# Self-attention on one NeuronCore: one exponential of two PSUM banks in place of two of one bank

## The chip, the cores and the metric

The kernel runs on 1 core of one Trainium2 chip. The metric is the device time of one execution in microseconds. Lower is better. Three runs of the kernel before gave 3151.02, 3143.84 and 3139.68 us, median 3143.84.

## What is computed

A decoder of two layers on x of 4 x 512 tokens x 512. Each layer is attention, cross-attention and feed-forward, each with a residual and a layer norm. The change is in the self-attention, which both layers have (`L0_attn`, `L1_attn`); it is one function, called twice:

```
x = _layernorm(x + _L0_attn_ref(x, ...))      # self-attention, layer 0
x = _layernorm(x + _L0_xattn_ref(x, ctx_512, ctx_512))
x = _layernorm(x + _L0_ffn_ref(x, ...))
x = _layernorm(x + _L1_attn_ref(x, ...))      # self-attention, layer 1
...
# self-attention, 16 heads of 32, B=4, S=512:
q, k, v = (split_heads(x @ W.T + b) for W, b in ((Wq, bq), (Wk, bk), (Wv, bv)))
scores = einsum('bhqd,bhkd->bhqk', q, k) * HEAD_DIM ** (-0.5)
scores = where(causal, scores, -inf)
out = einsum('bhqk,bhkd->bhqd', softmax(scores), v)
return out.reshape(B, S, HIDDEN) @ Wo.T + bo
```

## The kernel before, in words

`stage_self_attention` works in 16 groups n: batch element b = n // 4, and in it four heads, g = n % 4. One list, `plan` (lines 169 to 195), gives the order of all work, and each engine walks it and does its own part of each entry, in order. In the loop over groups, a group's entries are:

- `S n s`, s = 0 to 4: one **T unit**. TensorE writes scores, keys on the partitions, of the four heads into T, a PSUM tile of two banks of 512 columns (lines 487 to 500), and ScalarE takes them through the exponential to PT in SBUF (lines 298 to 307). `EXP_UNITS` (line 205) says which blocks of which head lie where; units 0 and 1 have two score matmuls, one a bank; the others have four, two a bank. Each score matmul (line 497) is followed by one that adds the causal mask (line 499).
- `M max (n+1, u)`, u = 0 to 5: a **maximum unit** of the next group. TensorE writes its scores, queries on the partitions, into one of two tiles M of two banks (lines 476 to 481), and VectorE reduces them to row maxima (line 375). These stand between the T units: two behind s=0, two behind s=1, one each behind s=2 and s=3.
- `M qk n+2`: the projections of the group after the next (line 422), taken from M by ScalarE (lines 291, 292) and VectorE (lines 364, 366) to HL, from which six DMAs of the SP queue and six of the POOL queue stack them to QKS (lines 221 to 223). `M mt n+1` transposes the maxima; a DMA of the ACT queue brings them to QKS (line 296).
- `P n 0..2`: the product of PT with V and with ones, into O and DEN (line 517). `Q`, `R`: VectorE's reciprocal of DEN and its multiplication (lines 393, 395), and the split of the result into two parts (lines 314, 399).
- in certain g, `xt` (transposed x), `v` (values) and `out` (output projection) units through M.

The last group, n=15, has no maximum units, so its five T units stand in a row. Groups 14 and 15 have no `qk` unit.

There is one tile T. Two semaphores pass it back and forth. TensorE, for each bank k of unit s:

```
t.wait_ge(t_free, 2 * (5 * n + s) + k + 1)
```

and it raises `t_full` behind the last matmul of each bank. ScalarE:

```
for k in range(2):
    bank = slice(BANK * k, BANK * (k + 1))
    act.wait_ge(t_full, 2 * (5 * n + s) + k + 1)
    ac.activation(PT[:, s, bank], T[:, bank], ACT.Exp, scale=SCALE).then_inc(t_free, 1)
```

Counts of `t_free` also release the PV products (line 509), and `t_full` the DMAs of HL (line 217). Both count two a unit.

Of the kernel before, what the change touches and what calls it, by code (L numbers as in the profile page):

```python
# [10 lines left out]
ACT = mybir.ActivationFunctionType  # L11
# [8 lines left out]
BANK = 512  # L20
# [90 lines left out]
def stage_self_attention(nc, tag, X, C, wts, bias_qk, bias_rows, x_src=None):  # L111
# [10 lines left out]
    SCALE = HD ** -0.5  # L122
    MOMENTS = NT + RSTD_STEPS
    pe, ve, ac, gp = nc.tensor, nc.vector, nc.scalar, nc.gpsimd
    ctx = ExitStack()
    with ctx:
# [12 lines left out]
        PT = sb("PT", [P, 5, 2 * BANK], F32)  # L139
# [12 lines left out]
        T = ps("T", [P, 2 * BANK])  # L152
# [8 lines left out]
        t_full, t_free = sem("t_full"), sem("t_free")  # L161
# [65 lines left out]
        @block.sync  # L227
        def _(sp):
            if x_src is not None:
                sp.dma_start(X[:, 0, :, :], x_src[:, 0, :, :]).then_inc(x_in, 16)  # L230
            sp.dma_start(WS[0], wts[0]).then_inc(w_in[0], 16)
            sp.dma_start(WS[1], wts[1]).then_inc(w_in[1], 16)
            sp.dma_start(BQK[:], bias_qk).then_inc(b_in, 16)
            sp.dma_start(BR[:], bias_rows).then_inc(b_in, 16)
            for w in range(2, 4):
                sp.wait_ge(w_lo, w - 1)
                sp.dma_start(WS[w % 2], wts[w]).then_inc(w_in[w % 2], 16)
            sp.wait_ge(ones_set, 2)
            for n in range(GROUPS):
                stack(sp, n, (0, 2))  # L240
                if x_src is not None and 1 <= n < NB:
                    sp.dma_start(X[:, n, :, :], x_src[:, n, :, :]).then_inc(x_in, 16)
# [25 lines left out]
        @block.scalar  # L268
        def _(act):
            act.sem_inc(t_free, 2)  # L270
            for x in plan:
                if x[0] == "W":
                    w = x[1]
                    act.wait_ge(w_in[w % 2], 16 * (w // 2 + 1))
                    ac.activation(WH[:, w], WS[w % 2], ACT.Copy).then_inc(w_hi, 1)
                elif x[0] == "M" and x[1] == "xt":
                    half = x[2][1]
                    act.wait_ge(m_full, at["xt", x[2]] + 1)
                    ac.activation(XTH[:, 2 * half:2 * half + 2, :].rearrange("p k s -> p (k s)"),
                                  M[at["xt", x[2]] % 2][:], ACT.Identity).then_inc(hi_done, 1)  # L280
                elif x[0] == "M" and x[1] == "qk":
                    n = x[2]
                    c = n % G
                    src = M[at["qk", n] % 2]
                    act.wait_ge(m_full, at["qk", n] + 1)
                    if n == 0:
                        act.wait_ge(b_in, 32)
                    else:
                        for arrived in stacked[(n - 1) % 2]:
                            act.wait_ge(arrived, 16 * 3 * ((n - 1) // 2 + 1))  # L290
                    ac.activation(HL[:, 1, :], src[:, 0:BANK], ACT.Identity, bias=BQK[:, 0, c:c + 1])
                    ac.activation(HL[:, 2, :], src[:, BANK:], ACT.Identity, bias=BQK[:, 1, c:c + 1]).then_inc(hi_done, 1)
                elif x[0] == "M" and x[1] == "mt":
                    n = x[2]
                    act.wait_ge(m_free, drained("mt", n))
                    act.dma_start(QKS[R:R + 1, n % 2, 0, :, :].bitcast(F32).rearrange("p h (i q) -> p (h i) q", i=NT),
                                  mT[:, :].bitcast(F32)).then_inc(shifted, 16)
                elif x[0] == "S":
                    n, s = x[1:]
                    if n == 0:  # L300
                        act.wait_ge(w_lo, 4)
                    else:
                        act.wait_ge(pv_part, 3 * (n - 1) + EXP_READER[s] + 1)
                    for k in range(2):
                        bank = slice(BANK * k, BANK * (k + 1))
                        act.wait_ge(t_full, 2 * (5 * n + s) + k + 1)
                        ac.activation(PT[:, s, bank], T[:, bank], ACT.Exp, scale=SCALE).then_inc(t_free, 1)  # L307
                elif x[0] == "Q":
                    n = x[1]
                    b, g = n // G, n % G  # L310
                    act.wait_ge(o_free, n + 1)
                    if b >= 1:
                        act.wait_ge(m_full, at["out", (b - 1, 1)] + 1)
                    ac.activation(ATH[:, g, :], AQ[:], ACT.Identity).then_inc(at_hi, 1)
# [1825 lines left out]
```

## Time and profile before

| | |
|---|---|
| median of 3 runs | 3143.84 us (3139.68 to 3151.02) |
| the profiled execution, its own time | 3156.45 us |
| its span, first to last instruction | 3154.7 us |
| mean granted clock of TensorE | 0.825 of full |
| busy: TensorE matmul / weight load | 2211.2 us / 1507.4 us |
| busy: VectorE / ScalarE / GpSimd | 1897.6 us / 1173.2 us / 527.9 us |
| the exponentials of self-attention | 320, 179.2 us busy, 596 ns each |
| TensorE waiting for them | 5.9 us, 16 times |

Times are from the start of the span. Engines are PE (TensorE matmul), PEld (its weight load), DVE (VectorE), ACT (ScalarE), POOL (GpSimd) and SP. A group of instructions is given with its line in the kernel, out<-in tiles, form, count, busy time and the mean of one, and then the engine's idle time before it with what ended it. In a timeline "x2" is two instructions that follow each other, shown as one with their common length; the matmuls' ends are modelled. The granted clock is 1.00 at full and 0.50 at half.

### The profile page before, as it was taken

To read this page: it belongs to the slowest core of one execution; us is meant where nothing else is said; L and a number is where in the kernel's file an instruction comes from. 1 tells how busy PE (TensorE), PEld (TensorE's weight loads), DVE (VectorE), ACT (ScalarE), POOL (GpSimd) and SP (SyncE) were. 2 spreads that over 40 slices of the span, in tenths; PEclk is the share of its full clock that TensorE was granted. 3 is DMA by queue.
4 is the path that set the end of the run, shared out by engine and by line. 5 is a ranking of instruction groups with operands and counts; after the bars stand their busy time and mean duration, and the time that the engine had idled before them with its cause. 6 is when DMAs were issued, how large, how long until landed. Compare 5 with 4: busy or idle time off the path is not lost. (4 is left out here: it accounts for less than half of the span.)

```text
span 3154.7 us, 35002 instructions
## 1 busy us (share of the span) xinstructions
PE 2211.2 (70%) x12378; PEld 1507.4 (48%) x12410; DVE 1897.6 (60%) x3060; ACT 1173.2 (37%) x2000; POOL 527.9 (17%) x498
## 2 busy tenths in 40 slices
PE   6999997578788328888848999995001638777770
PEld 5777775222222115555427777772001627655550
DVE  3355555578778556666653455554888343488876
ACT  2222221266666423333322222221785112255550
POOL 1112122101011000000001112211000040266654
PEclk7798998699999669999966889897555569999995
DMA  4222120521321210000012212210000200399875
GB/s 127 68 61 61 41 61 21 129 64 36 78 63 37 107 67 0 0 0 0 0 61 60 61 41 61 61 41 15 0 0 0 96 1 0 129 305 303 300 240 160
DMA packets 79911, 233.25 MB, mean 74 GB/s; under 512 B 16688, under 2 KB 17968, under 8 KB 70960
## 3 DMA queue, kind: packets, MB, share of 16 engines
q0 software_dynamic: 23552, 121.67, 12.9%
q1 hardware_dynamic: 55216, 109.70, 12.4%
q8 instruction: 78, 1.28, 0.2%
q10 hardware_dynamic: 1024, 0.26, 0.0%
q14 instruction: 41, 0.34, 0.0%
HBM read 149.23 MB, written 31.50 MB: 57 GB/s over the span
## 5 line engine op out<-in xcount | busy, mean ns | idle before, releaser
L773 DVE TENSOR_REDUCE x_negm<-x_M 128x2 f32<-128x1024 f32 x256 | 309.0, 1224 | 78.8 <-PE x_M L833 78.0
L307 ACT ACTIVATE L_attn_PT<-L_attn_T 128x512 f32<-128x512 f32 x320 | 179.2, 596 | 461.9 <-PE L_attn_T L499 461.8
L729 ACT ACTIVATE x_PT<-x_T 128x512 f32<-128x512 f32 x512 | 278.5, 598 | 185.2 <-PE x_T L853 179.9
L375 DVE TENSOR_REDUCE L_attn_negm<-L_attn_M 128x2 f32<-128x1024 f32 (+1 forms) x192 | 195.4, 1044 | 169.5 <-PE L_attn_M L480 169.0
L478 PE MATMUL L_attn_M<-L_attn_QKS 96*128 96x256 f32 (+3 forms) x512 | 195.5, 439 | 49.6 <-DMA L_attn_QKS<-L_attn_HL 27.4
L497 PE MATMUL L_attn_T<-L_attn_QKS 97*128 97x384 f32 (+3 forms) x512 | 193.2, 436 | 12.5 <-DMA L_attn_QKS<-L_attn_mT 10.5
L853 PE MATMUL x_T<-x_QS,x_KS 49*128 49x512 f32 x512 | 137.1, 532 | 46.7 <-ACT x_PT L729 41.6
L1310 PE MATMUL graph_P<-ident,graph_L 128*128 128x128 f32 x64 | 15.7, 427 | 214.0 <-DVE graph_L L1383 208.7
L221 POOL DMA_DIRECT2D L_attn_QKS<-L_attn_HL x64 | 34.8, 543 | 747.5 <-DVE L_attn_mT L379 669.0
L478 PEld LDWEIGHTS L_attn_M<-L_attn_QKS 96*128 96x128 f32 x512 | 123.4, 241 | 71.7 <-DVE L_attn_negm L375 15.1
L862 PE MATMUL x_O<-x_PT,x_V 128*32 128x512 f32 x1024 | 150.3, 662 | 8.3 <-issue 8.3
L1331 ACT ACTIVATE graph_seen_a<-graph_SIM,graph_mid 128x512 bf16<-128x512 f32 x200 | 141.4, 709 | 34.6 <-DVE graph_mid L1363 34.6
L833 PE MATMUL x_M<-x_KS,x_QS 48*128 48x512 f32 x512 | 114.8, 446 | 39.6 <-DVE x_negm L773 20.3
L853 PEld LDWEIGHTS x_T<-x_QS,x_KS 49*128 49x128 f32 x512 | 51.0, 196 | 189.5 <-ACT x_PT L729 136.0
L480 PE MATMUL L_attn_M<-mask_qk,identr 128*128 128x128 f32 x512 | 138.5, 276 | 0.0
L499 PE MATMUL L_attn_T<-mask_kq,identr 128*128 128x128 f32 x512 | 136.4, 274 | 0.0
L1366 DVE TENSOR_SCALAR_CACHE_REDUCE graph_seen_v<-graph_SIM,graph_mid 128x512 bf16<-128x512 f32 x200 | 135.3, 742 | 0.9
L1859 ACT ACTIVATE slots_WH<-slots_RAW 128x1024 fp32r<-128x1024 f32 x94 | 94.6, 1054 | 110.8 <-DMA slots_RAW<-in_experts,slots_PICK 110.8
L497 PEld LDWEIGHTS L_attn_T<-L_attn_QKS 97*128 97x128 f32 x512 | 123.7, 242 | 20.3 <-DMA L_attn_QKS<-L_attn_mT 12.1
L1920 DVE TENSOR_TENSOR slots_WL<-slots_RAW,slots_WH 128x1024 fp32r<-128x1024 f32 x48 | 128.7, 2681 | 0.2 <-ACT slots_WH L1871 0.2
L499 PEld LDWEIGHTS L_attn_T<-mask_kq,identr 128*128 128x128 f32 x512 | 125.0, 244 | 0.2
L480 PEld LDWEIGHTS L_attn_M<-mask_qk,identr 128*128 128x128 f32 x512 | 124.8, 244 | 0.3
(365 smaller groups left out, 5462.6 us busy)
## 6 DMA issues: line engine op xcount, KB each, us to landing
L_attn_QKS<-L_attn_HL SPq DMA_DIRECT2D x192, 128.0 KB, 4.8
L_attn_QKS<-L_attn_HL POOLq DMA_DIRECT2D x192, 128.0 KB, 3.7
moe_y_rows<-slots_YS SPq DMA_DIRECT2D x48, 256.0 KB
x_QS<-x_xh SPq DMA_DIRECT2D x128, 64.0 KB
X<-in_x SPq DMA_DIRECT2D x4, 1024.0 KB
x_xh<-x_XTH SPq DMA_DIRECT2D x4, 1024.0 KB, 3.9
x_xl<-x_XTL SPq DMA_DIRECT2D x4, 1024.0 KB, 5.1
x_KS<-x_ch SPq DMA_DIRECT2D x32, 128.0 KB, 4.5
```

The lines of the kernel that those rows point to most:

```text
L307: ac.activation(PT[:, s, bank], T[:, bank], ACT.Exp, scale=SCALE).then_inc(t_free, 1)
L375: last = ve.tensor_reduce(negm[:, g % 2, h0:h0 + nh, i], src, AX.X, ALU.max, negate=True)
L478: pe.matmul(m[:, c:c + w], QKS[0:R, r, 0, h, P * i:P * (i + 1)], QKS[0:R, r, 1, h, 0:w], start=True, stop=False)
L480: last = pe.matmul(m[:, c + P * i:c + w], C["identr"][:], C["mask_qk"][:], start=False, stop=True)
L497: pe.matmul(T[:, c:c + w], QKS[0:R + 1, r, 1, h, P * j:P * (j + 1)], QKS[0:R + 1, r, 0, h, P * j:S], start=True, stop=False)
L499: last = pe.matmul(T[:, c:c + P], C["identr"][:], C["mask_kq"][:], start=False, stop=True)
L729: ac.activation(PT[:, s // 4, head(s), :], T[(STEPS_S * g + s) % 3][:], ACT.Exp, scale=SCALE).then_inc(t_free, 1)
L773: ve.tensor_reduce(negm[:, g % 2, u // 4:4:2, u % 4], m[:].rearrange("p (r k) -> p r k", r=2), AX.X, ALU.max, negate=True).then_inc(m_free, 1)
L853: pe.matmul(T[(STEPS_S * g + s) % 3][:], KS[rows, g % KV, P * j:P * (j + 1)], QS[rows, g % 4, head(s) % 2, :], start=True, stop=True).then ...
L862: last = pe.matmul(O[VW * h:VW * (h + 1), :], V[:, (g // KV) % 2, j, g % KV, :], PT[:, j, h, :], start=(j == 0), stop=(j == NT - 1))
L1331: inst = ac.activation(seen_a[:, t - DVE_TILES, :], SIM[:, t, :], ACT.Sign, scale=-1.0, bias=mid[:, t:t + 1], accum_out=count[:, t:t + 1])
L1366: inst = ve.tensor_scalar(seen_v[:, t, :], SIM[:, t, :], mid[:, t:t + 1], 0.0, ALU.is_ge, ALU.add, accum_out=count[:, t:t + 1])
```

## The change

ScalarE waits until both banks of a T unit are full, takes both with one exponential of 1024 columns, and adds 2 to `t_free` when it ends. What is computed is the same. TensorE's code, with its waits for each bank, stays as it is; as both counts now come together, the wait for the second bank is met with the first. Nothing else is changed.

```
--- before
+++ after
@@ -301,10 +301,8 @@
                         act.wait_ge(w_lo, 4)
                     else:
                         act.wait_ge(pv_part, 3 * (n - 1) + EXP_READER[s] + 1)
-                    for k in range(2):
-                        bank = slice(BANK * k, BANK * (k + 1))
-                        act.wait_ge(t_full, 2 * (5 * n + s) + k + 1)
-                        ac.activation(PT[:, s, bank], T[:, bank], ACT.Exp, scale=SCALE).then_inc(t_free, 1)
+                    act.wait_ge(t_full, 2 * (5 * n + s) + 2)
+                    ac.activation(PT[:, s, :], T[:], ACT.Exp, scale=SCALE).then_inc(t_free, 2)
                 elif x[0] == "Q":
                     n = x[1]
                     b, g = n // G, n % G
```

## Rows read from the trace of the kernel before

**Rows 1.** The page, part 2: busy tenths of the matmul engine and its granted clock, in 40 slices.

```profile
PE   6999997578788328888848999995001638777770
...
PEclk7798998699999669999966889897555569999995
```

**Rows 2.** Groups of instructions, then one line's view: line 307, line 279.

```profile
L307 ACT ACTIVATE L_attn_PT<-L_attn_T 128x512 f32<-128x512 f32 x320 | 179.2, 596 | 461.9 <-PE L_attn_T L499 461.8
...
L279 ACT ACTIVATE L_attn_XTH<-L_attn_M x16: 1004/1025/1046, 15.9 to 1982.3; 128x1024 fp32r<-128x1024 f32 x16
```

**Rows 3.** Timeline, group n=3, full clock: start us, us, engine, line, instruction.

```profile
169.46 0.39 PE L497 MATMUL L_attn_T<-L_attn_QKS 97*128 97x384 f32 x1
...
169.86 0.28 PE L499 MATMUL L_attn_T<-mask_kq,identr 128*128 128x128 f32 x1
...
170.23 1.08 ACT L307 ACTIVATE L_attn_PT<-L_attn_T 128x512 f32<-128x512 f32 x2 [1.89 <-PE L_attn_T L499]
...
170.37 0.27 PE L499 MATMUL L_attn_T<-mask_kq,identr 128*128 128x128 f32 x1
...
171.42 0.39 PE L497 MATMUL L_attn_T<-L_attn_QKS 97*128 97x384 f32 x1
...
171.64 0.22 PE L499 MATMUL L_attn_T<-mask_kq,identr 128*128 128x128 f32 x1
...
172.33 0.27 PE L499 MATMUL L_attn_T<-mask_kq,identr 128*128 128x128 f32 x1
...
173.34 0.34 PE L497 MATMUL L_attn_T<-L_attn_QKS 97*128 97x256 f32 x1
```

**Rows 4.** Timeline, group n=7 at the low clock.

```profile
286.06 0.63 PE L497 MATMUL L_attn_T<-L_attn_QKS 97*128 97x384 f32 x1
...
287.77 0.41 PE L499 MATMUL L_attn_T<-mask_kq,identr 128*128 128x128 f32 x1
...
288.22 0.60 ACT L307 ACTIVATE L_attn_PT<-L_attn_T 128x512 f32<-128x512 f32 x1 [0.30 <-PE L_attn_T L499]
...
289.69 0.63 PE L497 MATMUL L_attn_T<-L_attn_QKS 97*128 97x384 f32 x1
```

**Rows 5.** Timeline, the last group of layer 0, n=15.

```profile
507.01 0.50 PE L497 MATMUL L_attn_T<-L_attn_QKS 97*128 97x512 f32 x1
...
507.70 0.23 PE L499 MATMUL L_attn_T<-mask_kq,identr 128*128 128x128 f32 x1
...
508.33 0.50 PE L497 MATMUL L_attn_T<-L_attn_QKS 97*128 97x512 f32 x1 [0.40 <-ACT L_attn_PT L307]
...
508.98 1.08 ACT L307 ACTIVATE L_attn_PT<-L_attn_T 128x512 f32<-128x512 f32 x2 [0.22 <-PE L_attn_T L499]
...
509.63 0.44 PE L497 MATMUL L_attn_T<-L_attn_QKS 97*128 97x384 f32 x1 [0.26 <-ACT L_attn_PT L307]
...
509.91 0.22 PE L499 MATMUL L_attn_T<-mask_kq,identr 128*128 128x128 f32 x1
...
511.11 0.69 PE L497 MATMUL L_attn_T<-L_attn_QKS 97*128 97x384 f32 x1 [0.23 <-ACT L_attn_PT L307]
```

**Rows 6.** Timeline, group n=14, between its last T unit and its PV product.

```profile
497.09 3.35 DVE L393 RECIPROCAL L_attn_AQ<-L_attn_DEN 128x512 f32<-128x512 f32 x1
...
501.22 1.08 PE L517 MATMUL L_attn_DEN<-L_attn_PT,L_attn_ones 128*32 128x512 f32 x4 [3.63 <-DVE L_attn_AQ L395]
```

**Rows 7.** Stretches: busy us by engine, then granted clock, DMA share, GB/s.

```profile
310.15:336.75 26.60, 24.82 (x180) 19.30 (x178) 12.94 (x13) 7.32 (x13) 10.34 (x10) 1.00 0.37 84
424.05:456.89 32.84, 31.16 (x180) 25.16 (x178) 12.94 (x13) 7.65 (x13) 10.32 (x10) 0.79 0.30 67
...
511.00:515.00 4.00, 3.90 (x16) 3.79 (x16) 0.25 (x1) 2.33 (x5) 0.00 (x0) 0.50 0.00 0
164.30:168.10 3.80, 2.15 (x13) 1.78 (x12) 1.97 (x3) 1.68 (x4) 0.00 (x0) 1.00 0.77 198
```

**Rows 8.** Timeline, start of T unit s=4 in the last full-clock group, n=14 of layer 1.

```profile
2111.05 0.33 PE L497 MATMUL L_attn_T<-L_attn_QKS 97*128 97x256 f32 x1
```


## The prediction

> **What bounds the kernel now.** First the slices of the page [rows 1]. The change touches only the two self-attention stages. They lie in the first seven slices and in the 22nd to the 28th, and most of these show TensorE (PE) 9 tenths busy or more. So what sets the end there is the order in which PE gets through its own queue, and a change on ScalarE (ACT) is worth what it does to PE's waits. ACT itself is idle for 461.9 us in front of its exponentials, because it waits for PE [rows 2]: a cheaper exponential shortens nothing by itself. The question is when PE may write T again. The second line of the slices is the granted clock of PE. In these slices it lies between 0.6 and 0.9, so stretches at full clock and at half of it (2.4 and 1.2 GHz) alternate, and both must be costed.
>
> Then the timeline of one group at full clock, n=3 [rows 3]. Unit s=2 starts at 169.46. Its first bank is complete at 169.86+0.28 = 170.14, and ACT starts 0.09 later. Its second bank is complete at 170.37+0.27 = 170.64. PE starts the next unit, s=3, at 171.42 without a wait. The first bank had been free since 170.23+0.60 = 170.83, so that start had 0.59 us in hand. That slack is what the change spends.
>
> **The pieces.** Removed: in each of 32 groups, five pairs of 512-column exponentials. Added: 160 exponentials of 1024 columns. The duration of one is the first unknown. A pair lasts 1.08 us from first start to last end [rows 3], and the one can't be longer, since it reads the same columns without a second start. From below, 128x1024 from the same memory by the same engine takes 1.004 to 1.046 us with a median of 1.025 [rows 2]. I take 1.025, the nearest row. ACT saves 0.06 us a unit, 8.8 us in all, and I cost that at nothing, since it falls into its 461.9 us of idle.
>
> The Trainium skill (ScalarE: Activation LUTs, What ACT_TABLE_LOAD costs) has 186 ns and 0.833 ns a column for an activation with immediate scale. By it the wide one would take 1.04 us and each stall below would be 0.015 us longer, under 1 us over all.
>
> Moved: two points in time. The exponential starts when the second bank is complete, and the first bank is free at its end. From the last matmul's end in a unit to PE's next write of T the chain is then 0.09 (start, above) + 1.025 + 0.05. The 0.05 is read where PE already waits for ACT: an exponential that began at 508.98 and lasted 0.60 released the matmul of 509.63 [rows 5]. The sum is 1.165 us. A PE that has stood there also restarts with its weight load in the open: its first matmul is followed after 0.28 us (509.63 to 509.91) in place of 0.22 (171.42 to 171.64) [rows 3, 5], so 0.06 more for each wait.
>
> **Groups at full clock.** s=2 to s=3: 170.64 + 1.165 = 171.81 against a start at 171.42, a wait of 0.39, with the restart 0.45. s=3 to s=4: 172.33+0.27+1.165 = 173.77 against 173.34, 0.43, with the restart 0.49. Together 0.94 a group. From s=0 to s=1 and s=1 to s=2 two maximum units and a wait lie between, and the chain fits (where an output unit takes that wait away, it misses by some hundredths). The intervals of 1.96 and 1.92 us repeat in 17 of the 30 groups that have maxima in them, the last time with s=4 at 2111.05 [rows 3, 8].
>
> **Groups at low clock.** Last matmul 287.77+0.41 = 288.18, plus 1.165 = 289.35, against a start at 289.69 [rows 4]. 0.34 is left over: no wait in the other 13 groups.
>
> **Is it carried to the end?** What PE issues behind the wait comes later by all of it: the maximum unit, the qk product, the transposed maxima, and with them the DMAs from HL and mT that the next groups wait for. These all start from PE's own work, so the waits for them move along. One exception: in n=14 of each layer there is no qk product. PE waits 3.63 us for VectorE's (DVE's) reciprocal, which started at 497.09, behind the last maximum and not behind s=4 [rows 6]. The stall before s=4 vanishes there. So 15 groups by 0.94 is 14.1 us, and two by 0.5 is 1.0.
>
> **The last groups** (n=15) have no maxima, and T units follow each other directly. Now s=0 to s=1 takes 508.33-507.01 = 1.32, s=1 to s=2 1.30, s=2 to s=3 1.48 [rows 5]. After: writing time plus 1.165. Writing takes 507.70+0.23-507.01 = 0.92 for the units of four matmuls, and 170.64-169.46+0.06 = 1.24 for those of eight [rows 3, 5]. That gives 2.09, 2.09 and 2.41: 0.77, 0.79 and 0.93 more. For s=3 to s=4 I take 0.93 again. 3.4 a layer, 6.8 for both. At low clock writing is 288.18-286.06 = 2.12 and the interval 3.29, so 0.88 us for each such unit would come on top.
>
> **The clock.** At full clock the stretch from s=2 to s=4 is now unbroken; the change puts two pauses of 0.4 us into it. What that does to the clock the trace of before doesn't show, so it needs bounds. For a fall: in n=15 PE paused only 0.40, 0.26 and 0.23 us before units [rows 5], and the clock was 0.50 from 511 on [rows 7]. Against: from 164.3 to 168.1 PE was busy 2.15 of 3.80 us, and the clock stayed at 1.00 [rows 7]. A fall costs at most what it does in n=12 beside n=8, the same work: 32.84 against 26.60 us, 6.2 [rows 7]. One that comes as late as s=4 costs less; I take what one T unit with its maximum unit loses, (289.69-286.06)-(171.42-169.46) = 1.7 us [rows 3, 4]. Bounds: none of 15 groups (0) and all of them at 6.2 (93 us). I take three of fifteen, at 1.7: 5 us, near the lower end, as the maximum units stand between the pauses here and don't in n=15.
>
> **Sum.** 14.1 + 1.0 + 6.8 + 5 = 27 us. The profiled execution took 3156.45 us (span 3154.7), so it would become 3183. The median of the three runs is 12.6 lower, about two groups' falls of the clock, and I count from it: 3143.8 + 27 = **3171 us**, 0.9% slower. A measurement of this kernel can tell about 0.3% (9.4 us) from no change.
>
> **Rivals.**
> - *The clock falls widely* (12%). With pauses in each full-clock group, seven more of them run as n=12 does. Each costs 6.2 and spares the 0.49 of s=4: 22 + 7 x 5.7 = 62 us, 3206 us. For it: n=15. Against: 164.3 to 168.1, and that 17 groups hold the clock with larger pauses before s=2. The Trainium skill (TensorE: Matmul & The Clock Gate, A second HAM failure mode: psum-queue depth-cycling) describes this: PE idles briefly between groups of matmuls as it cycles through PSUM, and the clock swings between its two levels.
> - *The waits don't add up* (5%). PE already idles in every group, before s=1 and s=2, on landing DMAs and on DVE. If these waits end at times that PE's delay doesn't move, they take it in; it decides from 0.9 us a group, and 164.3 to 168.1 has 1.65 us of such idle. Only the last groups' 6.8 stay: 3151 us, not slower by what can be told. Against: every one of these DMAs starts from a PE product of the group before.
> - *Fewer falls of the clock* (5%). Of the twelve groups like n=3, 4, 7 and 8, three (n=7 and n=12 in layer 0, one in layer 1) ran at low clock with the same work as their neighbours. If moved starts keep all three at full clock, 3 x 6.2 comes back: 22 - 19 = 3, 3147 us; only with four or more would it be faster.
> - *The change doesn't bite* is excluded: s=3 can't be written before the one exponential ends.
>
> **Numbers.** Forecast 78%, its own range 3158 to 3186: below it the stalls alone (22) less 8, since the runs shown differ by 11; above it five more late falls (8) and last groups at low clock (7). The whole range takes in half of the first rival: **3155 to 3195**. Faster than 3134: 0.02, all from the third rival. Within 0.3%: 0.08, from the second and third. Slower: 0.90.
>
> **What would show it.** ACT: 160 activations of 128x1024 near 1.02 us. PE: a new wait for ACT on T of about 0.4 us, twice in a full-clock group, none in a low-clock one, and 0.8 to 1.2 us four times in each n=15; in sum some 20 us, from next to nothing. The interval s=2 to s=3 grows from 1.96 to 2.4 us, and at low clock stays at 3.63. Wrong would be: no such waits; or the waits with the stages' length unchanged (second rival); or groups of 32 us where 26 stood (first rival).

## The result and the profile after

The changed kernel took 3187.73 us (median of 20 runs, 3175.11 to 3198.18), the kernel before 3150.58 us beside it (20 runs, 3134.77 to 3189.02). The ratio is 1.0113, with a 95% interval of 1.0090 to 1.0137: 28 to 43 us slower, 36 in the middle. The profiled execution took 3184.73 us, that of before 3156.45. One profiled execution further below, that of the late start with a common release, was over 1.5% slower than the fastest of its kernel, so only the timeline of one group at full clock is read from it.

The page of the changed kernel, its span, busy times, slices, and the group of the exponentials:

```profile
span 3183.0 us, 34842 instructions
...
PE 2224.5 (70%) x12378; PEld 1510.5 (47%) x12410; DVE 1898.4 (60%) x3060; ACT 1157.4 (36%) x1840; POOL 527.0 (17%) x498
...
PE   6999997478888428888848999995101648877770
...
PEclk7799998599899669999966798897655568999995
...
L305 ACT ACTIVATE L_attn_PT<-L_attn_T 128x1024 f32<-128x1024 f32 x160 | 163.8, 1024 | 517.7 <-PE L_attn_T L497 469.4
```

The slices are those of [rows 1] to within a tenth, and the mean granted clock is again 0.825. The 320 exponentials of 596 ns [rows 2] are 160 of 1024 ns; ScalarE is busy 15.8 us less and idle in front of them for longer. The view of the tile T says who now waits for them (min, median and max of one in ns; then us and times):

```profile
L305 ACT ACTIVATE L_attn_PT<-L_attn_T x160: 1018/1024/1027, 64.7 to 2163.7; 128x1024 f32<-128x1024 f32 x160
...
  PEld L_attn_T L495: 26.2, 43
  PE L_attn_T L495: 19.0, 42
```

The matmul engine waits 19.0 us for them, 42 times; before it was 2.0 us, 7 times. (The 5.9 us and 16 times in the table of before are the sum of two lines of this kind: 2.0 us, 7 times of the matmul engine, and 3.9 us, 9 times of its weight load. They are the same pauses, seen twice, so 2.0 is the figure to set beside 19.0.) The timeline of group n=3, at full clock, answers to [rows 3]:

```profile
168.29 0.39 PE L495 MATMUL L_attn_T<-L_attn_QKS 97*128 97x384 f32 x1
...
169.20 0.27 PE L497 MATMUL L_attn_T<-mask_kq,identr 128*128 128x128 f32 x1
...
169.59 1.02 ACT L305 ACTIVATE L_attn_PT<-L_attn_T 128x1024 f32<-128x1024 f32 x1 [2.27 <-PE L_attn_T L497]
...
170.66 0.44 PE L495 MATMUL L_attn_T<-L_attn_QKS 97*128 97x384 f32 x1 [0.26 <-ACT L_attn_PT L305]
...
172.02 1.02 ACT L305 ACTIVATE L_attn_PT<-L_attn_T 128x1024 f32<-128x1024 f32 x1 [1.41 <-PE L_attn_T L497]
...
173.10 0.39 PE L495 MATMUL L_attn_T<-L_attn_QKS 97*128 97x256 f32 x1 [0.30 <-ACT L_attn_PT L305]
```

Unit s=2 starts at 168.29 and s=3 at 170.66: 2.37 us in place of 1.96. From s=3 to s=4 it is 2.44 in place of 1.92. Each time PE stands until the one exponential has ended (169.59+1.02 = 170.61) and starts 0.05 or 0.06 us later. The interval grows by more than the wait in brackets, 0.41 us against 0.26 in the first case. Before, the next unit started at 171.42, 0.15 us ahead of the modelled end of the matmul in front of it, and the view counts idle time only from that end. Group n=7 at low clock answers to [rows 4]:

```profile
286.72 0.63 PE L495 MATMUL L_attn_T<-L_attn_QKS 97*128 97x384 f32 x1
...
288.96 1.02 ACT L305 ACTIVATE L_attn_PT<-L_attn_T 128x1024 f32<-128x1024 f32 x1 [4.21 <-PE L_attn_T L497]
...
290.34 0.63 PE L495 MATMUL L_attn_T<-L_attn_QKS 97*128 97x384 f32 x1
```

290.34 - 286.72 = 3.62 us, as before, with no wait. In the last group of layer 0, which answers to [rows 5], the same chain is open four times:

```profile
514.31 0.50 PE L495 MATMUL L_attn_T<-L_attn_QKS 97*128 97x512 f32 x1
...
515.35 1.02 ACT L305 ACTIVATE L_attn_PT<-L_attn_T 128x1024 f32<-128x1024 f32 x1 [7.82 <-PE L_attn_T L497]
...
516.42 0.50 PE L495 MATMUL L_attn_T<-L_attn_QKS 97*128 97x512 f32 x1 [1.20 <-ACT L_attn_PT L305]
...
518.52 0.44 PE L495 MATMUL L_attn_T<-L_attn_QKS 97*128 97x384 f32 x1 [1.20 <-ACT L_attn_PT L305]
...
520.96 0.69 PE L495 MATMUL L_attn_T<-L_attn_QKS 97*128 97x384 f32 x1 [1.19 <-ACT L_attn_PT L305]
...
524.33 0.58 PE L495 MATMUL L_attn_T<-L_attn_QKS 97*128 97x256 f32 x1 [1.20 <-ACT L_attn_PT L305]
```

2.11, 2.10 and 2.44 us, and then 3.37 as the clock had fallen. Before, the four intervals were 1.32, 1.30, 1.48 and 1.97.

The stretch from group 3 to group 15, in both layers, busy us by engine (PE, PEld, DVE, ACT, POOL) and the granted clock; first before, then after:

```profile
163.50:507.01 343.51, 322.89 (x2254) 260.13 (x2252) 185.53 (x246) 91.76 (x158) 66.36 (x86) 0.91 0.24 54
1781.69:2123.35 341.66, 319.55 (x2255) 255.84 (x2253) 185.60 (x246) 91.44 (x158) 66.37 (x86) 0.92 0.24 55
sum 685.17, PE 642.44 PEld 515.97 DVE 371.13 ACT 183.20 POOL 132.73; mean PE 321.22 PEld 257.98 DVE 185.56 ACT 91.60 POOL 66.37
```

```profile
162.15:514.31 352.16, 328.83 (x2254) 262.09 (x2252) 185.47 (x246) 86.60 (x98) 66.39 (x86) 0.90 0.23 53
1801.76:2150.70 348.94, 323.79 (x2254) 258.07 (x2253) 185.52 (x246) 86.59 (x98) 66.38 (x86) 0.92 0.23 53
sum 701.10, PE 652.63 PEld 520.16 DVE 370.99 ACT 173.18 POOL 132.77; mean PE 326.31 PEld 260.08 DVE 185.50 ACT 86.59 POOL 66.39
```

16 us come from there. Eleven of these 24 groups run at full clock throughout in both traces, and each of the eleven takes 0.74 to 1.12 us more than before, 0.98 in the mean: the stalls of a group reach the start of the next. The last groups, from s=0 of group 15 to its s=4, take 10.0 and 11.0 us in place of 6.1 and 5.6: 9 us. These 25 us are most of what this pair of executions differs by (28.3 in the spans). The rest can't be told from scatter of stages that no kernel here changes: with the one execution named above left out, the traces with the order of before take 1169 to 1189 us from s=4 of layer 0's last group to layer 1's first T unit, and 994 to 1026 from s=4 of layer 1's last group to the end.

### The profile page after: what moved, and what is told of

It reads as the page before. It is cut to its first block and busy times, and to the rows that moved or that the text cites. A ratio compares the mean times of both kernels' runs of the same rounds, so it can differ in the third digit from the quotient of the medians.

```text
span 3183.0 us, 34842 instructions
## 1 busy us (share of the span) xinstructions
PE 2224.5 (70%) x12378; PEld 1510.5 (47%) x12410; DVE 1898.4 (60%) x3060; ACT 1157.4 (36%) x1840; POOL 527.0 (17%) x498
## 3 DMA queue, kind: packets, MB, share of 16 engines
q10 hardware_dynamic: 1024, 0.26, 0.0%
## 5 line engine op out<-in xcount | busy, mean ns | idle before, releaser
L305 ACT ACTIVATE L_attn_PT<-L_attn_T 128x1024 f32<-128x1024 f32 x160 | 163.8, 1024 | 517.7 <-PE L_attn_T L497 469.4
L1329 ACT ACTIVATE graph_seen_a<-graph_SIM,graph_mid 128x512 bf16<-128x512 f32 x200 | 141.4, 708 | 34.6 <-DVE graph_mid L1361 34.6
```

Source lines behind the costliest of these rows:

```text
L305: ac.activation(PT[:, s, :], T[:], ACT.Exp, scale=SCALE).then_inc(t_free, 2)
L1329: inst = ac.activation(seen_a[:, t - DVE_TILES, :], SIM[:, t, :], ACT.Sign, scale=-1.0, bias=mid[:, t:t + 1], accum_out=count[:, t:t + 1])
```

## The experiments

A ratio is to the kernel before, run beside it on the same chip, with its 95% interval. Theory A is the forecast's: the cost is the chain from a unit's last matmul to the next write of T, wherever PE has less work than that in between. It has two ingredients, a late start and a common release. The first three runs take them apart.

**Late start, each bank freed by itself.**

```
                     for k in range(2):
                         bank = slice(BANK * k, BANK * (k + 1))
-                        act.wait_ge(t_full, 2 * (5 * n + s) + k + 1)
+                        act.wait_ge(t_full, 2 * (5 * n + s) + 2)
```

> Two exponentials of 512 columns again, both started only when the unit's two banks are full, each bank freed at its own exponential's end. Theory A (what counts is the chain from the last matmul of a unit to the next write of T, 0.09 + exponential + 0.05): the first bank is free 0.74 us after the last matmul, which at full clock is just the 0.74 to 0.78 us that the maximum unit gives; intervals s=2 to s=3 to s=4 stay at 1.96 and 1.92 within 0.05 us, only the last groups grow by some 0.3 to 0.5 us a unit, 3 to 4 us in all; ratio 1.000 to 1.003. Rival B (the late start is what costs): the change's waits stay, intervals 2.4, ratio 1.008 to 1.013.

Ratio 1.0006 (0.9974 to 1.0039). Group n=3:

```profile
168.87 0.39 PE L497 MATMUL L_attn_T<-L_attn_QKS 97*128 97x384 f32 x1
...
170.16 1.09 ACT L307 ACTIVATE L_attn_PT<-L_attn_T 128x512 f32<-128x512 f32 x2 [2.16 <-PE L_attn_T L499]
...
170.83 0.42 PE L497 MATMUL L_attn_T<-L_attn_QKS 97*128 97x384 f32 x1
...
172.80 0.39 PE L497 MATMUL L_attn_T<-L_attn_QKS 97*128 97x256 f32 x1
```

The pair starts when the unit is complete, and yet s=3 starts 1.96 us behind s=2, and s=4 1.97 behind s=3, 0.05 more than before. In all the trace PE waits 6.0 us for ACT, all of it in the last groups, where s=0 to s=4 takes 8.9 and 8.4 us. That is 5.7 us more than before, where 3 to 4 were expected; the clock was at half for the last interval in both layers. Rival B is out: a late start alone costs next to nothing outside the last groups.

**Early start, both banks freed together.**

```
                         act.wait_ge(t_full, 2 * (5 * n + s) + k + 1)
-                        ac.activation(PT[:, s, bank], T[:, bank], ACT.Exp, scale=SCALE).then_inc(t_free, 1)
+                        last = ac.activation(PT[:, s, bank], T[:, bank], ACT.Exp, scale=SCALE)
+                    last.then_inc(t_free, 2)
```

> Two exponentials of 512 columns, each started when its bank is full as before, but both banks freed together at the end of the second. Theory A: the chain is again 0.74 us (the second exponential alone is behind the last matmul), intervals 1.96 and 1.92, last groups 0.3 us a unit longer, ratio 1.000 to 1.003. Rival C (freeing as a whole is what costs, however early the exponentials start): intervals 2.4, ratio 1.008 to 1.013.

Ratio 1.0022 (0.9994 to 1.0049). Group n=3:

```profile
167.56 0.39 PE L498 MATMUL L_attn_T<-L_attn_QKS 97*128 97x384 f32 x1
...
168.33 1.11 ACT L307 ACTIVATE L_attn_PT<-L_attn_T 128x512 f32<-128x512 f32 x2 [2.13 <-PE L_attn_T L500]
...
169.52 0.42 PE L498 MATMUL L_attn_T<-L_attn_QKS 97*128 97x384 f32 x1
...
171.48 0.38 PE L498 MATMUL L_attn_T<-L_attn_QKS 97*128 97x256 f32 x1
```

Again 1.96 and 1.96: the common release at 168.33+1.11 = 169.44 is just in time for 169.52. Rival C is out as well. Either ingredient alone fits into the slack at full clock. The last groups take 8.5 us each, 5.4 more together, where 0.3 us a unit was expected.

**Late start and common release, with two exponentials.** Both edits together:

```
-                        act.wait_ge(t_full, 2 * (5 * n + s) + k + 1)
-                        ac.activation(PT[:, s, bank], T[:, bank], ACT.Exp, scale=SCALE).then_inc(t_free, 1)
+                        act.wait_ge(t_full, 2 * (5 * n + s) + 2)
+                        last = ac.activation(PT[:, s, bank], T[:, bank], ACT.Exp, scale=SCALE)
+                    last.then_inc(t_free, 2)
```

> Two exponentials of 512 columns, both started when the unit is full and both banks freed at the end of the second: the change without the wide instruction. Theory A: chain 0.09 + 1.08 + 0.05 = 1.22 us, 0.06 more than in the change; intervals 2.44 to 2.50 at full clock and 3.63 at low clock, PE waits for ACT about 0.05 us longer each than in the change; ratio 1.010 to 1.014. Rival D (the 1024-column form itself costs): intervals back to 1.96, ratio under 1.004.

Ratio 1.0106 (1.0069 to 1.0143), that of the change. Group n=3:

```profile
167.89 0.39 PE L498 MATMUL L_attn_T<-L_attn_QKS 97*128 97x384 f32 x1
...
168.80 0.28 PE L500 MATMUL L_attn_T<-mask_kq,identr 128*128 128x128 f32 x1
...
169.18 1.08 ACT L307 ACTIVATE L_attn_PT<-L_attn_T 128x512 f32<-128x512 f32 x2 [2.19 <-PE L_attn_T L500]
...
170.32 0.44 PE L498 MATMUL L_attn_T<-L_attn_QKS 97*128 97x384 f32 x1 [0.30 <-ACT L_attn_PT L307]
...
172.79 0.39 PE L498 MATMUL L_attn_T<-L_attn_QKS 97*128 97x256 f32 x1 [0.33 <-ACT L_attn_PT L307]
```

2.43 and 2.47 us, with waits of 0.30 and 0.33 where the change has 0.26 and 0.30. So it is not the 1024-column form: two exponentials of 512, synchronised alike, cost the same and about 0.04 us more each time. Rival D is out. The 0.04 can be taken apart: the pair lasts 1.08 us against 1.02, but starts 0.10 us behind the last matmul (168.80+0.28 = 169.08 to 169.18) where the wide one starts 0.12 behind it.

**The wide exponential everywhere but in the last groups, and only there.** The diff is of the first, against the changed kernel, with changes of indentation alone left out; the second has n + 1 == GROUPS as its condition.

```
+                    if n + 1 < GROUPS:
                         act.wait_ge(t_full, 2 * (5 * n + s) + 2)
                         ac.activation(PT[:, s, :], T[:], ACT.Exp, scale=SCALE).then_inc(t_free, 2)
+                    else:
+                        for k in range(2):
+                            bank = slice(BANK * k, BANK * (k + 1))
+                            act.wait_ge(t_full, 2 * (5 * n + s) + k + 1)
+                            ac.activation(PT[:, s, bank], T[:, bank], ACT.Exp, scale=SCALE).then_inc(t_free, 1)
```

> The change in groups 0 to 14 of each layer, the code of before in group 15. Theory A: intervals of 2.4 us in the full-clock groups as in the change, last groups back at 1.3 to 1.5 us a unit (at full clock); that takes 8 to 10 us off the change, ratio to before 1.007 to 1.009. Rival E (the last groups' excess is taken in by what follows them): same time as the change, ratio 1.011.

> The wide exponential only in group 15 of each layer. Theory A: intervals 1.96 and 1.92 in all other full-clock groups; the last groups take about 10 and 11 us instead of 6 from s=0 to s=4; time 8 to 10 us over before, ratio 1.0025 to 1.0035. Rival E (taken in by what follows): 1.000.

Ratios 1.0095 (1.0065 to 1.0124) and 1.0050 (1.0019 to 1.0080). PE's waits for ACT, us in total, times, longest; first the kernel with the wide one outside the last groups, then the other:

```profile
PE L_attn_T L501 <- ACT L_attn_PT L306: 8.1, 28, 0.6
PE L_attn_T L501 <- ACT L_attn_PT L311: 1.8, 6, 0.4
```

```profile
PE L_attn_T L501 <- ACT L_attn_PT L306: 9.6, 8, 1.2
```

28 waits, 8.1 us in all, against 8 waits of 1.2 us. The last groups of the second take 11.0 and 10.9 us where before has 6.1 and 5.6, and the excess reaches the end: this run puts rival E out, since its interval lies above 1.000, though it doesn't say whether 6 or 25 us arrive. The other run alone would not have: its interval holds both the 1.007 to 1.009 of theory A and the 1.011 of rival E. Both ratios lie a little above what was expected, by amounts that their intervals cover.

**The change once more**, for a second trace of the clock. Its time was measured again too.

> The change itself once more, for a second trace of the granted clock. In one pair of traces the change and the kernel before had equally many groups at low clock (7 of the 16 groups with g other than 1 and n over 2), but the other two kernels with pauses at full clock had 10 each, those without had 4 and 7. Theory F (pauses make the clock fall in more groups): 8 to 10 of 16 here and one or more falls behind s=3; ratio 1.011. Rival G (the falls are chance): 4 to 8 of 16.

Ratio 1.0143 (1.0104 to 1.0181). For the clock, the 24 groups n=3 to n=14 of both layers were counted in each trace: those that run s=2 to s=4 at low clock (their interval is 3.62 or 3.63 us), and those that lose the clock only behind s=3, up to 1 us after s=4 starts. Group 14 needs this bound: in every kernel of the table its clock is also seen to fall 2 to 5 us after s=4 starts, pauses or not, and that is not counted. The late start with a common release is not in the table.

| kernel | pauses at full clock | low clock from s=2 | lost behind s=3 | groups 3 to 15, both layers |
|---|---|---|---|---|
| before | no | 7 | 0 | 685.2 us |
| late start | no | 4 | 0 | 668.0 us |
| common release | no | 7 | 0 | 684.3 us |
| wide only in group 15 | no | 5 | 0 | 672.6 us |
| the change | yes | 7 | 2 | 701.1 us |
| the change again | yes | 8 | 2 | 706.2 us |
| wide in all but group 15 | yes | 10 | 2 | 718.2 us |

A late fall is seen in each kernel with pauses and in none without. What it costs shows in group 13 of the change: in layer 0, where it came, the group took 33.8 us, and in layer 1, without it, 32.2. That is 1.6 us. In the second trace of the change one late fall cost the same 1.6 (group 9, 34.6 against 33.0), and one, which lasted twice as long, 3.2 (group 13, 35.4 against 32.2). For the falls ahead of s=2, the second trace gave 8, which lies in the range of theory F (8 to 10) and in that of rival G (4 to 8). All in all 7 to 10 against 4 to 7 lean towards theory F without settling it, and the next two pairs of runs show how far one order of work scatters: 0 and 4 such groups in two traces. The falls ahead of s=2 come before the pauses of their own group, and why a pause in one group should bring the clock down in a later one no run here shows.

**Another order: the work that covers the chain.** The maximum unit u=5 goes in front of s=3 and the qk product in front of s=4, once with the exponentials of before, once with the wide one in groups 0 to 14:

```
-            plan += [("S", n, 3)] + maxima(5) + [("S", n, 4)]
+            plan += maxima(5) + [("S", n, 3)]
             plan += [("Q", n - 1)] if n else []
             plan += [("M", "qk", n + 2)] if n + 2 < GROUPS else []
+            plan += [("S", n, 4)]
```

> The kernel before with another order only: the maximum unit u=5 stands before s=3 and the qk product before s=4. It is the control for the next run. If PE's order alone is neutral, ratio 0.998 to 1.002. As the qk product starts about 1 us earlier, the DMAs of HL land earlier and PE's wait for them behind s=0 (1.1 us in a group) may shrink: at best 20 us less, ratio 0.993.

> The same order with the wide exponential in groups 0 to 14 (group 15 as before). Now more than 1.8 us of PE's work lies between s=2 and s=3 and over 5 us between s=3 and s=4, against a chain of 1.165. Theory A: PE's waits for ACT vanish in groups 0 to 14, and the time equals that of the order with two exponentials within 0.2%. Rival H (something else in the wide exponential costs, such as its later end for ACT's own queue): still 0.5% or more over the order with two.

Ratios 0.9811 (0.9765 to 0.9856) and 0.9835 (0.9785 to 0.9885): both beat the kernel before, by some 60 and 50 us. PE's waits with two exponentials, then with the wide one (line 307 there is the wide one), and at last the wait of before that shrank:

```profile
PE L_attn_M L479 <- DMA L_attn_QKS<-L_attn_HL: 10.7, 11, 2.1
...
PE L_attn_T L498 <- ACT L_attn_PT L308: 2.5, 9, 0.4
```

```profile
PE L_attn_M L483 <- DMA L_attn_QKS<-L_attn_HL: 9.1, 9, 2.1
...
PE L_attn_T L502 <- ACT L_attn_PT L307: 2.4, 2, 1.2
```

```profile
PE L_attn_M L478 <- DMA L_attn_QKS<-L_attn_HL: 27.4, 25, 2.2
```

With the wide exponential nothing is left of its waits but two of 1.2 us: group 14 of each layer has no qk product, so s=3 and s=4 are neighbours there. (The rest of that view, 2.0 us in 7 waits, is for the exponentials of 512 in group 15, as before.) Apart from that case, which the expectation had overlooked, theory A holds: put more of PE's work into the interval and the wait is gone. The order itself was to be neutral or worth 20 us at best; it is worth 59 of 3148, and that with two exponentials, which had hardly a wait to lose. The traces show two things that it gives. One is the wait for the stacked heads, 27.4 us before (21.6 to 27.4 in the traces with the old order) and 10.7 now. The other, and the larger, is the clock: seven groups fewer at half clock, at the 6.2 us between n=12 and n=8 [rows 7], would be 43 us, an estimate. The stretch from group 3 to group 15 of layer 0, with PE's busy time and its clock:

```profile
161.20:472.06 310.86, 297.19 (x2255) 0.99 0.26 59
```

310.9 us at 0.99, where before has 343.5 at 0.91. Layer 1 takes 309.3 us for the same groups, and the two together 620 us in place of 685. Not one of the 24 groups n=3 to n=14 of both layers runs s=2 to s=4 at low clock; with the wide exponential one does. Which part of the order holds the clock up was not taken apart.

**The last groups too.** In group 15 the product of the first units goes before s=3 and that of the next before s=4, on top of the new order, with two exponentials and with the wide one in groups 0 to 14:

```
+            if last:
+                plan += [("S", n, 0), ("S", n, 1), ("S", n, 2), ("Q", n - 1), ("R", n - 1), ("P", n, 0),
+                         ("S", n, 3), ("P", n, 1), ("S", n, 4), ("P", n, 2)]
+                continue
             plan += [("S", n, 0)]
```

> The new order (u=5 before s=3, qk before s=4) with the exponentials of before, and in group 15 of each layer the product of the first units before s=3 and that of the next before s=4. The five T units of group 15 then no longer stand in a row: two of the four waits of 0.2 to 0.4 us go, and the exponential of s=4 is waited for before the last product, about 0.7 us. Expected within 3 us of the new order alone: ratio 0.980 to 0.982 to before. It is here to see whether the last groups hold anything to be had.

> The same with the wide exponential in groups 0 to 14. Theory A: the chain of 1.165 us is covered everywhere, so the time is that of order_last within 0.2%; no group from n=3 to n=14 at low clock (theory F, since no pause is left between s=2 and s=4). Rival H: 0.5% or more slower than order_last.

Ratios 0.9795 (0.9752 to 0.9838) and 0.9834 (0.9783 to 0.9885). Neither can be told from the same order without it. Clean of the low clock they were not: the trace with two exponentials has four of the 24 groups at low clock and the other has one. The order of these 24 groups is in both that of the runs above, so with two exponentials the same order had no such group in one trace and four in another. The wide exponential was the slower one in both pairs, by 0.24% and 0.40%. Of that, its two waits in group 14 account for some 1.9 us, or 0.06%: the interval from s=3 to s=4 is 2.38 us there in place of 1.43. With intervals of half a per cent that is neither rival H's half per cent nor the expected 0.2%, and it stays open.

## Why the prediction was right

The time lies in the whole range of 3155 to 3195, and the direction and the mechanism are those forecast. The forecast was 27 us, just below the interval of 28 to 43 with 36 in its middle. The forecast's own, narrower range ended at 3186 and the time is 3188; 7 us of the distance from 3171 are in the kernel before, whose median was 3143.8 in three runs and 3150.6 in twenty.

- **The duration of the wide exponential**: taken as 1.025 us from the row of another 128x1024 activation, measured 1.024 (1.018 to 1.027). That it relieves ScalarE and that this is worth nothing held too: 15.8 us less busy, where 8.8 was forecast, and nothing gained. The busy time of its group fell by 179.2 - 163.8 = 15.4 us. The 8.8 took every pair for 1.08 us long. In the trace of before, 42 of the 160 pairs don't touch, since the second bank was full only after the first exponential had ended ([rows 4] show one such unit), and these are 1.19 us busy.
- **The chain**: 1.165 us forecast. In group n=3 it runs from 169.20+0.27 = 169.47 to 170.66, 1.19 us. The 0.03 more lies ahead of the exponential, whose start was taken from one of 512 columns: in all the trace the wide ones that had waited for PE start 0.116 to 0.119 us behind the last matmul of their unit, and those of 512 in the trace of before, in the median, 0.097 behind that of their bank.
- **Full-clock groups**: 2.41 us forecast for each of the two intervals, measured 2.37 and 2.44, together 0.93 more than before where 0.94 was forecast. The trace has 17 such groups again. In the two of n=14 a part was to vanish in the wait for the reciprocal, and that wait fell from 7.3 us to 5.7, and to 6.4 in the second trace of the change. The view's own waits were forecast too long, 0.4 us against 0.26 and 0.30, since they count from the matmul's modelled end; that their sum of 19.0 met "some 20" is partly luck, because the last groups gave 9.6 of it.
- **Low-clock groups**: no wait forecast, none found.
- **Is it carried**: yes. The eleven groups at full clock in both traces grew by 0.98 us in the mean, and the three kernels with a wide exponential or a late, common release in groups 0 to 14, measured four times, came out 0.95% to 1.43% slower.
- **The last groups**, 6.8 us forecast, measured 9.3 (10.0+11.0 against 6.1+5.6). The first three intervals of layer 0 came as worked out, 2.11, 2.10 and 2.44 against 2.09, 2.09 and 2.41. The term was too small because the clock was down in three of the eight intervals, the one behind s=3 in layer 0 and those behind s=2 and s=3 in layer 1. Each took 3.37 or 3.38 us, where 2.41 was in the sum. The prediction held this for possible at 0.88 us a unit and left it out.
- **The clock**, the term sized by choice between far bounds: three late falls at 1.7, 5 us. Late falls came, two in each trace that pauses, at 1.6 us or, once, 3.2, where the cost could be read. That the guess lay so near is luck, as nothing in the trace of before spoke for three rather than none or fifteen. Full falls ahead of s=2 were not in the term. The four traces without pauses have 5.75 of them in the mean and the change's two 7.5. As the same order of work gave 0 and 4 in two traces, this is no measured effect.

So the mechanism and the stalls' price were right, and the last groups' term was 2.5 us too small. What the pair of traces accounts for is 16 + 9 = 25 us, beside a forecast of 27. Where the rest up to the 36 of the twenty runs comes from stays open; more falls of the clock are the candidate, without a count that shows them. The rival of the widely falling clock asked for seven more groups at low clock, 14 in place of 7; the traces show 7, 8 and 10. The rule of the Trainium skill named beside it (TensorE: Matmul & The Clock Gate, A second HAM failure mode: psum-queue depth-cycling) agrees in kind: kernels with brief pauses between PE's groups lost the clock behind s=3, two groups in each trace, and the same work without pauses in none of four. The clock also falls without them, in 4 to 7 groups a trace, which no run here explains. The waits that "don't add up" are refuted by the eleven groups above, and by all four measurements, of which the lowest bound is 1.0065. The "fewer falls" rival has no trace that speaks for it.

## What to carry to other kernels

A merged instruction on a buffer with a single copy is not costed by its own time but by the chain from the producer's last write to its next one: late start, whole duration, hand-over. Set that against the producer's own work in between, at the clock at which this work is shortest; either a late start or a common release may still fit where both together don't. And before changing the consumer, look whether work of the producer's own can be moved into the interval: here that removed all but two of the wide exponential's waits in groups 0 to 14 and was worth more than either form of it.

## What the hardware showed that had not been expected

The wide exponential began 0.12 us after the last matmul's modelled end (169.47 to 169.59), the narrow one 0.10 us (169.08 to 169.18 in the late start with a common release). The 0.02 us is seen in every trace that has both forms. So of the 0.06 us by which one instruction is shorter than the pair, 0.04 is left.

How long PE runs at low clock differs by more than the pauses put in. Groups 3 to 15 of both layers took 668 to 685 us with no pause, 17 us apart with the same order of work. With two pauses in some 15 of the 24 groups they took 701 to 718, on average 31 us more, where the pauses themselves put in about 15. With the order changed and two exponentials they took 620 us in one trace, with no group at low clock between s=2 and s=4, and 643 in another with four.
